# Routing one-hots of a mixture-of-experts layer: every operand 16-bit in SBUF, the four choices innermost

## The reference

```
x = x + 0.5 * moe(layernorm(x))
x = x + scan_layer(layernorm(x))
x = x + 0.5 * moe(layernorm(x))

def moe(x):                                  # 16 experts, 4 choices per token, hidden width 176
    scores = sigmoid(gate_w @ x) + gate_b
    weights, indices = top_k(scores, 4); weights /= weights.sum(-1)
    shared = silu(x @ w1s) * (x @ w3s) @ w2s
    routed = sum over the 4 choices of  weight * (silu((x @ w1[e]) * (x @ w3[e])) @ w2[e])
    return shared + routed
```

## Time and profile before

| | us |
|---|---|
| median of 3 runs (lowest, highest) | 695.64 (693.73, 697.45) |
| the profiled execution | 695.84 |
| its span | 693.6 |
| TensorE busy, share of the span | 499.8, 72% |
| VectorE busy | 439.3, 63% |
| ScalarE busy | 380.8, 55% |
| GpSimd busy | 351.7, 51% |
| first pick to start of the gathers, first layer | 56.16 to 76.88 |
| the same, second layer | 410.29 to 431.58 |

### The profile page before, as it was taken

One profiled execution on the slowest core, in us unless ns is written; L12 is line 12 of the kernel. 1 busy time (PEld: TensorE's weight loads), 2 busy tenths in 40 slices (PEclk: granted clock), 3 DMA queues, 4 the chain that ended last, 5 costly groups with the idle time before them and its releaser, 6 DMA issues.

```text
span 693.6 us, 14287 instructions
## 1 busy us (share of the span) xinstructions
PE 499.8 (72%) x3218; PEld 457.2 (66%) x3219; DVE 439.3 (63%) x1448; ACT 380.8 (55%) x1153; POOL 351.7 (51%) x358
## 2 busy tenths in 40 slices
PE   4877599999999912657677887899999999600000
PEld 3855499999999911446456765899999999500000
DVE  6679377777777715577854687477777777324334
ACT  3587377777777721456563556577777777400000
POOL 2399544444444247777404141544444444177774
PEclk9989699999999965787887987799999999855555
DMA  8963334444444433434102421344444445344553
GB/s 276 328 238 105 127 103 136 130 127 136 130 130 127 112 121 108 127 114 122 53 1 89 141 96 54 106 126 133 136 126 131 136 126 131 107 136 136 158 161 96
DMA packets 61520, 89.88 MB, mean 130 GB/s; under 512 B 9564, under 2 KB 46684, under 8 KB 61492
## 3 DMA queue, kind: packets, MB, share of 16 engines
q1 hardware_dynamic: 47667, 51.78, 21.9%
q0 software_dynamic: 13824, 37.77, 21.6%
HBM read 58.06 MB, written 31.46 MB: 129 GB/s over the span
## 4 chain that ended last, share of the span: by engine, by line
PE 52%; POOL 14%; issue 13%; DMA 8%; DVE 8%; ACT 3%; DVEq 1%; SPq 0%; POOLq 0%; ACTq 0%
PE bank L974 25%; POOL mamba_room L402 14%; PE bank L1024 13%; PE bank L996 5%; DMA mamba_room<-ys_scratch,si 3%; PE bank L1034 3%; PE bank L1035 2%; DVE xres L834 2%; DMA ys_scratch<-ring_f 1%; DMA ring_f<-xn_scratch,tokidx 1%; DMA raw_routed<-in_w2r 1%; DVE ring_f L809 1%; DMA xn_scratch<-ring_f 1%; PE bank L1106 1%; PE bank L1079 1%
## 5 line engine op out<-in xcount | busy, mean ns | idle before, releaser
L392 POOL DMA_INDIRECT ring_f<-xn_scratch,tokidx x160 | 152.6, 954 | 165.3 <-PE bank L996 154.1
L974 PE MATMUL bank<-w_routed,ring_r 128*128 x960 | 197.5, 341 | 0.1
L402 POOL DMA_INDIRECT mamba_room<-ys_scratch,si x128 | 131.0, 1024 | 73.0 <-issue 36.3
L974 PEld LDWEIGHTS bank<-w_routed,ring_r 128*128 128x128 f32 x960 | 154.8, 193 | 0.6 <-issue 0.5
L1024 PE MATMUL bank<-w_routed,ring_r 128*128 x800 | 121.2, 282 | 0.8 <-DVE ring_r L699 0.5
L834 DVE SCALAR_TENSOR_TENSOR xres<-mamba_room,wk,xres 128x256 f32<-128x256 f32 (+1 forms) x128 | 53.4, 478 | 96.2 <-DMA mamba_room<-ys_scratch,si 96.2
L1024 PEld LDWEIGHTS bank<-w_routed,ring_r 128*128 128x128 f32 x800 | 111.5, 188 | 1.9 <-issue 1.9
L462 ACT ACTIVATE ring_r<-bank 128x256 fp32r<-128x256 f32 x160 | 61.6, 385 | 74.1 <-PE bank L1035 73.9
L697 DVE TENSOR_TENSOR ring_r<-bank,ring_r 128x128 fp32r<-128x128 f32 x160 | 46.7, 292 | 64.1 <-ACT ring_r L462 64.1
L689 DVE TENSOR_TENSOR ring_r<-bank,ring_r 128x256 fp32r<-128x256 f32 x160 | 68.0, 425 | 16.7 <-ACT ring_r L454 11.8
L996 PE MATMUL bank<-cst,ring_f 128*128 128x128 f32 x320 | 63.1, 280 | 8.0 <-DMA ring_f<-xn_scratch,tokidx 8.0
(11 more groups left out here) (129 smaller groups left out, 754.1 us busy)
## 6 DMA issues: line engine op xcount, KB each, us to landing
ys_scratch<-ring_f SPq DMA_DIRECT2D x160, 128.0 KB, 2.3
raw_routed<-in_w13r SPq DMA_DIRECT2D x6, 704.0 KB, 5.0
xn_scratch<-ring_f SPq DMA_DIRECT2D x32, 128.0 KB, 2.2
shared_scratch<-ring_f SPq DMA_DIRECT2D x32, 128.0 KB, 1.7
mamba_room<-shared_scratch SPq DMA_DIRECT2D x32, 128.0 KB, 2.3
raw_routed<-in_w2r SPq DMA_DIRECT2D x6, 512.0 KB, 6.8
raw_routed<-in_w13r SPq DMA_DIRECT2D x8, 352.0 KB, 4.6
ring_f<-xn_scratch,tokidx POOLq DMA_INDIRECT x160, 2.9
```

The costliest lines, as they stand in the source:

```text
L392: pool.indirect_dma_start(xg[j % UN], None, xn_dram, bass.IndirectOffsetOnAxis(ap=tokidx[:, j:j + 1], axis=0)).then_inc(s_g[j % UN], 16)
L402: pool.indirect_dma_start(cg[t % 4][:, q, :], None, ys_dram, bass.IndirectOffsetOnAxis(ap=si[:, n:n + 1], axis=0)).then_inc(s_cg[t % 4], 16)
L974: last = pe.matmul(out, a, b, start=(q == 0), stop=(q == len(terms) - 1))
```

## The change

- The index copy goes to SBUF as fp16 (`if4`) in place of PSUM as fp32, and the slot numbers' two parts get a further copy from PSUM int32 to SBUF fp16 (`lohi`, 128 columns).
- The constant becomes `i4`, each of 0..127 four times in a row, and `oh`, `prod`, `pickA` and `pickB` have the four choices innermost. So in the three comparisons all of in0, in1 and out are fp16 in SBUF, with contiguous groups of four at least. The number of columns is the same.
- ScalarE reads `pickB` with a step of four elements and writes `pickS` contiguously. TensorE reads `oh` (as moving operand of `count`) and `pickA` (as weights of the picks) with a step of four elements, 8 bytes. The sum over the experts (L797, now L801) reads `prod` with a step of four fp32.
- `te` moves from a tensor of its own into a piece of `stage[1]`. The constants' load is 768 instead of 464 columns of fp16.

```diff
-H_TRI, H_ONE, H_I128, H_INS = 0, 128, 256, 384
-NHCST = 384 + NS
+H_TRI, H_ONE, H_I4 = 0, 128, 256
+NHCST = H_I4 + TOPK * P
...
-        oh = ring_h[:, 2048:3072].rearrange("p (t k e) -> p t k e", t=NT, k=TOPK)
-        prod = ring_f[:, 0:1024].rearrange("p (t k e) -> p t k e", t=NT, k=TOPK)
-        pickA = [ring_h[:, b * 512:(b + 1) * 512].rearrange("p (k s) -> p k s", k=TOPK) for b in range(3)]
+        oh = ring_h[:, 2048:3072].rearrange("p (t e k) -> p t e k", t=NT, k=TOPK)
+        prod = ring_f[:, 0:1024].rearrange("p (t e k) -> p t e k", t=NT, k=TOPK)
+        pickA = [ring_h[:, b * 512:(b + 1) * 512].rearrange("p (s k) -> p s k", k=TOPK) for b in range(3)]
...
-        pickB, pickS = ([picks[b].rearrange("p (k s) -> p k s", k=TOPK) for b in (h, h + 2, 4 + h)] for h in range(2))
+        pickB, pickS = ([picks[b].rearrange(o, k=TOPK) for b in (h, h + 2, 4 + h)]
+                        for h, o in enumerate(("p (s k) -> p s k", "p (k s) -> p k s")))
...
+        i4 = hcst[:, H_I4:].rearrange("p (s k) -> p s k", k=TOPK)
...
-                link(dve.tensor_copy(p_if4.rearrange("p (t k) -> p t k", k=TOPK), i8[:, :, 0:TOPK]))
-                ie = cst[:, C_IE:C_IE + NE]
-                dve.tensor_tensor(oh.rearrange("p t k e -> p (t k) e"),
-                                  p_if4.unsqueeze(2).broadcast_to((P, NT * TOPK, NE)),
-                                  ie.unsqueeze(1).broadcast_to((P, NT * TOPK, NE)), ALU.is_equal).then_inc(s_mem, 1)
+                link(dve.tensor_copy(if4, i8[:, :, 0:TOPK]))
+                dve.tensor_tensor(oh, if4.unsqueeze(2).broadcast_to((P, NT, NE, TOPK)),
+                                  i4[:, 0:NE, :].unsqueeze(1).broadcast_to((P, NT, NE, TOPK)), ALU.is_equal
+                                  ).then_inc(s_mem, 1)
...
-                link(dve.tensor_tensor(prod, oh, sl.unsqueeze(2).broadcast_to((P, NT, TOPK, NE)), ALU.mult))
-                link(dve.tensor_reduce(p_slotf, prod.rearrange("p t k e -> p (t k) e"), AX.X, ALU.add))
+                link(dve.tensor_tensor(prod, oh, sl.unsqueeze(3).broadcast_to((P, NT, NE, TOPK)), ALU.mult))
+                link(dve.tensor_reduce(p_slotf.rearrange("p (t k) -> p t k", k=TOPK), prod.rearrange("p t e k -> p t k e"), AX.X, ALU.add))
...
+                link(dve.tensor_copy(lohi, p_lohi))
...
-                dve.tensor_tensor(pickB[t % 3], hcst[:, H_INS:H_INS + NS].unsqueeze(1).broadcast_to((P, TOPK, NS)),
-                                  p_hii[:, q].unsqueeze(2).broadcast_to((P, TOPK, NS)), ALU.is_equal).then_inc(s_pkb, 1)
-                dve.tensor_tensor(pickA[t % 3], hcst[:, H_I128:H_I128 + P].unsqueeze(1).broadcast_to((P, TOPK, P)),
-                                  p_loi[:, q].unsqueeze(2).broadcast_to((P, TOPK, P)), ALU.is_equal).then_inc(s_pka, 1)
+                dve.tensor_tensor(pickB[t % 3], i4[:, 0:NS, :], hi.broadcast_to((P, NS, TOPK)), ALU.is_equal
+                                  ).then_inc(s_pkb, 1)
+                dve.tensor_tensor(pickA[t % 3], i4, lo.broadcast_to((P, P, TOPK)), ALU.is_equal).then_inc(s_pka, 1)
...
-                    pe.matmul(p_pre, hcst[:, H_TRI:H_TRI + P], oh[:, :, k, :], start=(k == 0), stop=(k == TOPK - 1))
+                    pe.matmul(p_pre, hcst[:, H_TRI:H_TRI + P], oh[:, :, :, k], start=(k == 0), stop=(k == TOPK - 1))
...
-                    last = pe.matmul(p_tok, pickA[t % 3][:, k, :], pickS[t % 3][:, k, :],
+                    last = pe.matmul(p_tok, pickA[t % 3][:, :, k], pickS[t % 3][:, k, :],
```

More of the change, by code:

```diff
@@ L128, in build @@
         wk = sb("wk", [P, NT * TOPK])
-        te = sb("te", [1, NS], i32)
         tokidx = sb("tokidx", [P, NS], i32)
@@ L133, in build @@
         r1 = lambda a, b: rt[1][:, a:b]
+        te = r1(880, 880 + NS)[0:1, :].bitcast(i32)
         v8 = r0(0, 128).rearrange("p (t k) -> p t k", k=8)
@@ L136, in build @@
         wsum = r0(320, 336)
+        lohi = r0(1040, 1104).bitcast(f16)
+        if4 = r0(1104, 1136).bitcast(f16).rearrange("p (t k) -> p t k", k=TOPK)
         rawlg = r1(0, 256)
@@ L171, in build @@
         p_sig, p_exc, p_slot = pb[1][:, 256:512], pb[1][:, 256:512], pb[1][:, 0:256]
-        p_if4, p_rw = pb[1][:, 0:64], pb[1][:, 64:80]
+        p_rw = pb[1][:, 64:80]
         p_cnt, p_ntl, p_ctl = pb[1][:, 128:144], pb[1][:, 144:160], pb[1][:, 160:176]
@@ L176, in build @@
         p_si, p_loi, p_hii = p_si.bitcast(i32), p_loi.bitcast(i32), p_hii.bitcast(i32)
+        p_lohi = pb[0][:, 128:256].bitcast(i32)
         p_pre, p_tot, p_tok, p_te = (pb[0][:, 0:NT * NE], pb[0][:, NT * NE:2 * NT * NE], pb[1][:, 0:NS],
@@ L527, in scale_pick @@
                     act.wait_ge(s_pkd, f * NT + t - 2)
-                act.activation(pickS[t % 3], pickB[t % 3], ACT.Copy, scale=cst[:, C_TOK + t:C_TOK + t + 1]
+                act.activation(pickS[t % 3], pickB[t % 3].rearrange("p s k -> p k s"), ACT.Copy, scale=cst[:, C_TOK + t:C_TOK + t + 1]
                                ).then_inc(s_pk, 1)
@@ L784, in route_slots @@
                 link(dve.scalar_tensor_tensor(off, tbx, float(P), ge3[:, :, 0], ALU.mult, ALU.subtract))
-                dve.tensor_tensor(teq[0:NE, :], hcst[0:NE, H_INS:H_INS + NS], p_ctc[0:NE, :].broadcast_to((NE, NS)),
+                dve.tensor_tensor(teq[0:NE, :], i4[0:NE, 0:NS, 0], p_ctc[0:NE, :].broadcast_to((NE, NS)),
                                   ALU.is_ge)
@@ L805, in pick @@
                     dve.wait_ge(s_pkd, f * NT + t - 2)
-                q = slice(t * TOPK, (t + 1) * TOPK)
-                dve.tensor_tensor(pickB[t % 3], hcst[:, H_INS:H_INS + NS].unsqueeze(1).broadcast_to((P, TOPK, NS)),
-                                  p_hii[:, q].unsqueeze(2).broadcast_to((P, TOPK, NS)), ALU.is_equal).then_inc(s_pkb, 1)
-                dve.tensor_tensor(pickA[t % 3], hcst[:, H_I128:H_I128 + P].unsqueeze(1).broadcast_to((P, TOPK, P)),
-                                  p_loi[:, q].unsqueeze(2).broadcast_to((P, TOPK, P)), ALU.is_equal).then_inc(s_pka, 1)
+                lo = lohi[:, t * TOPK:(t + 1) * TOPK].unsqueeze(1)
+                hi = lohi[:, (NT + t) * TOPK:(NT + t + 1) * TOPK].unsqueeze(1)
+                dve.tensor_tensor(pickB[t % 3], i4[:, 0:NS, :], hi.broadcast_to((P, NS, TOPK)), ALU.is_equal
+                                  ).then_inc(s_pkb, 1)
+                dve.tensor_tensor(pickA[t % 3], i4, lo.broadcast_to((P, P, TOPK)), ALU.is_equal).then_inc(s_pka, 1)
             def route_end(f):
@@ L1091, in count @@
                 for k in range(TOPK):
-                    pe.matmul(p_pre, hcst[:, H_TRI:H_TRI + P], oh[:, :, k, :], start=(k == 0), stop=(k == TOPK - 1))
+                    pe.matmul(p_pre, hcst[:, H_TRI:H_TRI + P], oh[:, :, :, k], start=(k == 0), stop=(k == TOPK - 1))
                 for k in range(TOPK):
-                    last = pe.matmul(p_tot.rearrange("p (e t) -> p t e", e=NE), hcst[:, H_ONE:H_ONE + P], oh[:, :, k, :],
+                    last = pe.matmul(p_tot.rearrange("p (e t) -> p t e", e=NE), hcst[:, H_ONE:H_ONE + P], oh[:, :, :, k],
                                      start=(k == 0), stop=(k == TOPK - 1))
@@ L1200, in _constants @@
     h[:, H_ONE:H_ONE + P] = 1.0
-    h[:, H_I128:H_I128 + P] = np.arange(P)
-    h[:, H_INS:H_INS + NS] = np.arange(NS)
+    h[:, H_I4:] = np.repeat(np.arange(P), TOPK)
     return c, h
```

## The result

The changed kernel takes 708.0 us (median of 4 runs, 706.75 to 710.53), the kernel before 696.55 beside it (4 runs, 693.73 to 698.95): a ratio of 1.018, interval 1.015 to 1.022. The span is 706.0 us in place of 693.6. Slower, 1 us from the forecast.

The account below looks back on a forecast made before the run. A ring of TensorE and ScalarE was taken to pace the picks; comparisons moved to SBUF would take turns with GpSimd's subtractions on the shared port: 695.84 + 11.0 (first layer) + 2.2 (second) = 709.0 us, range 695 to 716.

Parts of the forecast that it names:

- The ring paces, VectorE does not: Pick stage: TensorE and ScalarE, waiting on each other, need 1.13 us a pick, VectorE 1.00; faster comparisons buy nothing.
- Double rate at 0.42, 0.32, 0.68: VectorE's comparisons of 512, 320 and 1024 columns, all 16-bit in SBUF, drop from 0.681, 0.484 and 1.224 us.
- `oh` -0.54 a layer: Members' comparison, the only one on a chain (TensorE waits for it in the second layer): 0.54 us less a layer.
- Sum over experts +0.7, copy +0.3: VectorE ahead of the picks: strided sum and copy to `lohi` add +1.0 us together, inside its 2.6 us lead.
- 8-byte steps at nothing: Strided reads by TensorE's weight loads, `oh` and ScalarE's scaling: taken as free; other bound +0.21 us for ScalarE's 320 columns.
- The rival that charged 7 us for them: Steps cost on top of the turns, at L791's rate in ScalarE's scaling and weight loads: 716 us, chance 0.1.
- Turns: Two-SBUF-input comparisons and GpSimd's subtractions alternate on the shared port by whole instructions, each comparison waiting for one; chance 0.5, 704 to 714.
- Runs keep the port: Rival: closely spaced VectorE instructions keep GpSimd waiting; its long row ends near 79; 699.5 us, chance 0.2.
- No contention: Rival: 16-bit comparisons leave the shared port to GpSimd; only `oh`, twice -0.54, remains; 694.8 us, chance 0.2.
- The size of a turn: Contended pick: two 1.45 us subtractions plus comparisons' port time (duration less 0.13): 3.4 us against the ring's 1.13.
- First layer, +11.0 forecast: Picks start near 58.5, 9 to 10 comparisons (5 picks) pass by 74.7, sixth pick ready at 75.3 + 0.1: +11.0 us.
- Second layer, +2.2 forecast: Three comparisons in turns against GpSimd's six subtractions, third pick at 416.6 against 414.40: +2.2 us.

Follow-up runs that it names:

- the port free: Kernel before and changed kernel, GpSimd writing zeros where it subtracted: 720.05 and 720.58 us; both with the hidden tile turned ahead of the pick: 715.32 and 712.45.
- TensorE's order alone: Kernel before, comparisons untouched, TensorE turning a step's hidden tile ahead of the pick instead of behind it: 719.93 us, ratio 0.9912 to the kernel before.
- at single rate: Kernel before, its old layout (choices outermost), with all operands of the three comparisons fp16 in SBUF: 712.2 us, ratio 1.0225 to the kernel before.
- one turn a pick: Changed kernel with `pickB`'s second input in PSUM, so only `pickA` has both inputs in SBUF: 734.55 us, ratio 1.0133 to the kernel before.
- old order: Changed kernel as it is, TensorE turning the hidden tile behind the pick: 708.0 us, ratio 1.018 to the kernel before.
- new order: Changed kernel with TensorE turning the hidden tile ahead of the pick: 738.12 us, ratio 1.0150 to the kernel before.

## Why the prediction was right, and where it was off

**The ring paces, VectorE does not:** right. With the port free the comparisons were at 0.32 and 0.42, and the whole change bought about 1 us by the timelines, nothing that the times can tell; TensorE's order alone bought 6.4 (3.8 to 9.1).

**Double rate at 0.42, 0.32, 0.68:** right: 0.41 to 0.42, 0.31 to 0.32, 0.69. `oh` -0.54 a layer: right in the second (1.22 to 0.69), where it met an idle GpSimd; in the first it waited, as the prediction had it.

**Sum over experts +0.7, copy +0.3:** 2.09 against 1.23, +0.86, somewhat more than L791's rate gives, though the steps are 16 bytes and not 64; the copy +0.29.

**8-byte steps at nothing:** nearly. Means by form of ScalarE's scaling after the change, to be held against 0.55:

```profile
L533 ACT ACTIVATE ring_f<-ring_f,cst 128x320 f16<-128x320 f16 x22 | 12.4, 576 | 5.7 <-DVE ring_f L813 5.7
```

+0.02 us a pick, and a weight load takes 114 ns in place of 96 (medians). The rival that charged 7 us for them is out: with the layout of the change and the second input in PSUM, both layers together were +0.85 us, and with the port free the whole change was -0.8.

**Turns:** right. Each comparison waited for one subtraction while GpSimd had work, and each subtraction came through after it. The Trainium skill (SBUF — State Buffer, Who interferes with whom) says that a VectorE instruction with two SBUF inputs contends with a GpSimd one that reads SBUF; these runs agree for 16-bit operands as well, at double rate (1.89) and at single rate (1.75), and with one input in PSUM nothing waited (0.68). *Runs keep the port* is out: GpSimd's long row ended at 72.57, not near 79. *No contention* is out by the first long comparison.

**The size of a turn** was the term that was off. I let a comparison hold the port for its duration less 0.13, 3.4 us a pick; measured 3.13. Two subtractions take 2 x 1.453 = 2.91, which leaves 0.22 for two comparisons of 0.73 together: each holds it for its duration less some 0.26. The other two runs fit that: at single rate 2.91 + (1.16 - 0.52) = 3.55, measured 3.54; with one turn a pick, two picks take 2.91 + 2 x (0.41 - 0.26) = 3.21, measured 3.23. By this estimate the hand-over happens 0.13 ahead of the record's end on both sides; I had counted one of them.

**First layer, +11.0 forecast, +10.6 measured,** out of two misses that cancel. Ahead of the picks I had +2.3 us, and it was +3.2 (60.93 - 45.41 = 15.5 against 56.16 - 43.84 = 12.3): index copy +1.1, `oh` +0.9, sum +0.9, `lohi` +0.3; the index copy waited for most of a subtraction and not for half. From the first pick to the gather I had +8.7, and it was +7.4, by the shorter turns and because 8 comparisons got through in turns, not 9 to 10: GpSimd's row ended at 72.57, where the longer turns had it end at 74.7. That this layer came out within 0.4 us is luck; the mechanism is not.

**Second layer, +2.2 forecast, +1.7 measured:** +0.6 ahead of the picks (I had +0.5) and +1.1 behind.

## What to carry to other kernels

Before a `tensor_tensor` is made faster by moving its second input from PSUM to SBUF, look in the timeline for GpSimd instructions beside it: here a comparison of 0.42 us that had to wait for a subtraction cost 1.6. And first ask who waits for the instruction at all: here the whole change, with nobody in its way, was worth about 1 us in 700, and a few lines of TensorE's order 6. Where a stage runs as a ring of two engines, look for the engine whose short step (the turned tile) the other needs and that stands behind a long one; take that out before anything is sped up beside the ring.

## What was unexpected in the hardware

- A stretch of waiting is followed by a lower clock. The windows of the changed kernel's first layer, picks in turns and picks behind them, and then of the kernel before, its picks in two parts:

```profile
60.00:73.00 13.00, 6.24 (x36) 4.23 (x35) 12.90 (x14) 4.06 (x10) 12.57 (x9) 0.72 0.30 99
73.00:88.00 15.00, 11.97 (x83) 8.66 (x83) 7.33 (x24) 10.49 (x25) 1.28 (x1) 0.73 0.13 45
```

```profile
56.00:64.00 8.00, 6.85 (x49) 4.87 (x48) 7.38 (x16) 5.19 (x15) 8.00 (x6) 1.00 0.50 163
64.00:76.00 12.00, 8.38 (x70) 5.72 (x70) 9.03 (x18) 8.88 (x22) 8.86 (x7) 0.92 0.16 55
```

  TensorE waits up to 2.8 us for a pick, and its granted clock is 0.72 and 0.73, in the kernel before 1.00 and 0.92. In the old order that costs little (sixth to 16th pick 11.5 us against 11.2, since the ring waits for ScalarE anyway), in the new order all that the order had bought.
- A read with innermost steps of 16 bytes, fp32, costs VectorE's reduction 0.83 ns a column (2.09 against 1.23 us for 1024), not less than the 64-byte steps of L791; 8-byte steps of 16-bit numbers cost TensorE's weight load 18 ns and ScalarE 0.02 us for 320 columns. The Trainium skill (SBUF — State Buffer, Door 1: The DMA port swizzle) has SBUF in lines of 16 bytes, of which at least two accesses must hit for full speed; the first cost agrees with it; the second, with two numbers to a line, is small but not nothing, which is not quite what it says.
- While both engines always have an instruction waiting they alternate strictly: between the 8 contended comparisons of the changed kernel's first layer, and between the 11 of the old-layout one's, there lies one subtraction each time, never none and never two.
